# The inverse standard deviation of nine layer norms: Ln and Exp on rows, or Sqrt and reciprocal on tokens

## The chip, the cores and the metric

One core of one Trainium2 chip runs the whole program in one launch. The metric is the device time of that core in microseconds (us), the median of the runs. Engines are named as in the profile: PE (TensorE), PEld (its weight loads), DVE (VectorE), ACT (ScalarE), POOL (GpSimd) and SP (SyncE).

## The reference, cut to what matters

A small transformer-like network over 4 x 1024 tokens of 128 features. Each of its eight blocks is added to the residual and takes a layer norm of it without gain or bias; one norm more, over 256 features, sits inside the seventh block.

```python
def _layernorm(x, axis=-1, eps=1e-05):
    m = jnp.mean(x, axis=axis, keepdims=True)
    v = jnp.var(x, axis=axis, keepdims=True)
    return (x - m) / jnp.sqrt(v + eps)

x = x + _L0_attn_ref(_layernorm(x), ...)   # attention, 16 heads of 8, softmax
x = x + _L0_ffn_ref(_layernorm(x), ...)    # mixture of experts, the best 2 of 8
x = x + _L1_attn_ref(_layernorm(x), ...)   # attention
x = x + _L1_ffn_ref(_layernorm(x), ...)    # experts with a capacity, best 1 of 8
x = x + _L2_attn_ref(_layernorm(x), ...)   # state-space scan
x = x + _L2_ffn_ref(_layernorm(x), ...)    # mixture of experts, the best 2 of 16
x = x + _L3_attn_ref(_layernorm(x), ...)   # scan; inside: yn = (y - mu) / sqrt(var + 1e-05) * ln_g + ln_b
x = x + _L3_ffn_ref(_layernorm(x), ...)    # squared relu, then five spike steps
```

## The kernel before

The residual lies in SBUF as `g.xT`, features on the 128 partitions and the 4096 tokens along them; a norm writes `g.xn`. The program is a series of stages (class `Stage`), each with semaphores and PSUM of its own, and each is one `nc.Block()`: one instruction list per engine, run in the order written, and a barrier of all engines at its end. The order inside a stage is written by hand; nothing plans it.

`norm_stage` is called nine times: n0 to n7 with one source tile (k = 1), n0 ahead of the first attention, n1 and n3 ahead of the expert stages `f0r` and `f1r`, n5 ahead of `f2r`; and `m3n` with two source tiles (k = 2), in place. Tokens are cut into eight chunks of 512 (`CH`), these into two halves m of four chunks q. Features are on the partitions, so sums over them are matmuls:

- `mean(c)`, L172: a 128x128 matrix of 1/(128 k) times chunk c puts the mean on all 128 partitions of a PSUM bank; three banks in turn.
- centring, L216 on DVE: source minus mean, into the destination.
- `square(c)`, L227 on ACT.
- `variance(m)`, L179 on PE: four matmuls with 32 output columns each, so that chunk q of the half has its variance on the 32 partitions of group q (the same row 32 times) of one bank.
- `inverse_root(m)`, ACT: L231 takes the Ln of variance plus eps, 128x512 out of PSUM, and L233 the Exp of minus one half of it, into `inv`.
- `broadcast(m)`, L190 on PE: four matmuls, a one-hot column of the identity against the 32 partitions of group q, spread the row of chunk q over 128 partitions. Half 0 goes to banks 5, 6, 7, 0, half 1 to banks 1 to 4.
- `scale(m)`, L211 on DVE: destination times these banks, 4 k multiplies of 128x512.

PE's order is `mean` 0 to 5, `variance(0)`, `mean` 6 and 7, `broadcast(0)`, `variance(1)`, `broadcast(1)`. DVE has the eight centrings, then `scale(0)`, `scale(1)`. ACT has squares 0 to 5, `inverse_root(0)`, squares 6 and 7, `inverse_root(1)`. Ahead of that ACT is told to load a table set that holds both functions, and warms it:

```python
act.preload_act_table_set("natural_log_exp_and_others")   # L235
act.activation(warm[:, :], g.eps[:, :], ACT.Ln).then_inc(table, 1)   # L236
```

Other loads of tables are placed by the compiler in front of an ACTIVATE whose function the set then loaded lacks. Outside the norms these lines use `Exp` first: L642 (a warm-up at the head of each of the two attention stages), L1153 (`f0r`), L1634 (`f1r`), L924 and L925 (`f2r`). L1328 is the first `Silu` of the stage behind `f0r`.

Other lines that the text speaks of: L822, `f0r` and `f1r`, transposes of 128x128 f32 on PE, four to a PSUM bank, read by DVE at L836; L133, a DVE copy of 128x512 f32 from PSUM; L903, a DVE reciprocal of 128x32.

Of the kernel before, what the change touches and what calls it, by code (L numbers as in the profile page):

```python
# [13 lines left out]
ACT = mybir.ActivationFunctionType  # L14
# [4 lines left out]
P = 128  # L19
BATCH, SEQ = 4, 1024  # L20
TOK = BATCH * SEQ
CH = 512
NCH = TOK // CH
# [113 lines left out]
def norm_stage(nc, g, name, src=None, dst=None, ahead=()):  # L137

    src, dst = src or [g.xT[:, :]], dst or [g.xn[:, :]]
    k = len(src)
    with Stage(nc, name) as s:
        sq = s.sb("sq", [P, k, TOK])
        mean_w = s.sb("mean_w", [P, P])
        log, inv, warm = s.sb("log", [P, 2, CH]), s.sb("inv", [P, 2, CH]), s.sb("warm", [P, 1])
        ps = s.ps("ps", [P, 8, CH])
        bank = lambda i: ps[:, i, :]
        mean_ps, var_ps = [bank(i) for i in range(3)], [bank(3), bank(4)]
        spread = [[bank(i) for i in (5, 6, 7, 0)], [bank(i) for i in (1, 2, 3, 4)]]  # L150
        w_ready, mean_ready, centred, squared = (s.sem(x) for x in ("w_ready", "mean_ready", "centred", "squared"))
        var_ready, log_done, inv_done, inv_spread, scaled, table = (
            s.sem(x) for x in ("var_ready", "log_done", "inv_done", "inv_spread", "scaled", "table"))
        cols = lambda c: slice(c * CH, (c + 1) * CH)
        group = lambda q: slice(32 * q, 32 * q + 32)
        with nc.Block() as block:
            @block.sync
            def _(sp):
                for weights in ahead:
                    weights.load(sp)  # L160

            @block.gpsimd
            def _(pool):
                pool.memset(mean_w[:, :], 1.0 / (k * P)).then_inc(w_ready, 1)  # L164

            @block.tensor
            def _(pe):
                def mean(c):
                    if c >= 3:
                        pe.wait_ge(centred, k * (c - 2))  # L170
                    for i in range(k):
                        mm = pe.matmul(mean_ps[c % 3], mean_w[:, :], src[i][:, cols(c)], start=i == 0, stop=i == k - 1)  # L172
                    mm.then_inc(mean_ready, 1)

                def variance(m):
                    pe.wait_ge(squared, 4 * k * (m + 1))
                    for i in range(k):
                        for q in range(4):
                            mm = pe.matmul(var_ps[m][group(q), :], mean_w[:, 0:32], sq[:, i, cols(4 * m + q)],  # L179
                                           start=i == 0, stop=i == k - 1)  # L180
                    mm.then_inc(var_ready, 1)

                def broadcast(m):
                    pe.wait_ge(inv_done, m + 1)
                    if m == 0:
                        pe.wait_ge(centred, k * 7)
                    else:
                        pe.wait_ge(centred, k * NCH)
                    for q in range(4):
                        mm = pe.matmul(spread[m][q], g.ident[group(q), 32 * q:32 * q + 1].to_broadcast([32, P]),  # L190
                                       inv[group(q), m, :], start=True, stop=True)
                    mm.then_inc(inv_spread, 1)

                pe.wait_ge(w_ready, 1)
                for c in range(6):
                    mean(c)
                variance(0)
                mean(6)
                mean(7)
                broadcast(0)  # L200
                variance(1)
                broadcast(1)

            @block.vector
            def _(dve):
                def scale(m):
                    dve.wait_ge(inv_spread, m + 1)
                    for q in range(4):
                        for i in range(k):
                            x = dst[i][:, cols(4 * m + q)]  # L210
                            dve.tensor_tensor(x, x, spread[m][q], ALU.mult).then_inc(scaled, 1)  # L211

                for c in range(NCH):
                    dve.wait_ge(mean_ready, c + 1)
                    for i in range(k):
                        dve.tensor_tensor(dst[i][:, cols(c)], src[i][:, cols(c)], mean_ps[c % 3], ALU.subtract).then_inc(centred, 1)  # L216
                dve.wait_ge(centred, k * NCH)
                scale(0)
                scale(1)
                dve.wait_ge(scaled, k * NCH)  # L220

            @block.scalar
            def _(act):
                def square(c):
                    for i in range(k):
                        act.wait_ge(centred, k * c + i + 1)
                        act.activation(sq[:, i, cols(c)], dst[i][:, cols(c)], ACT.Square).then_inc(squared, 1)  # L227

                def inverse_root(m):
                    act.wait_ge(var_ready, m + 1)  # L230
                    act.activation(log[:, m, :], var_ps[m], ACT.Ln, bias=g.eps[:, :]).then_inc(log_done, 1)  # L231
                    act.wait_ge(log_done, m + 1)
                    act.activation(inv[:, m, :], log[:, m, :], ACT.Exp, scale=-0.5).then_inc(inv_done, 1)  # L233

                act.preload_act_table_set("natural_log_exp_and_others")  # L235
                act.activation(warm[:, :], g.eps[:, :], ACT.Ln).then_inc(table, 1)  # L236
                for c in range(6):
                    square(c)
                inverse_root(0)
                square(6)  # L240
                square(7)
                inverse_root(1)


def store_stage(nc, g, out):
# [549 lines left out]
class Logits:  # L795
# [34 lines left out]
    def take(self, dve, link, L):  # L830
        for m in range(2):
            dve.wait_ge(self.logits, m + 1)
            for q in range(4):
                t = 16 * m + 4 * q
                from_q = self.tok_ps[:, m, :].rearrange("p (j q r) -> p q j r", q=4, r=32)[:, q, :, 0:self.e]
                last = dve.tensor_copy(L[:, t:t + 4, :], from_q)  # L836
            link(last)
# [1748 lines left out]
def build(nc, a, out):  # L2586
    with ExitStack() as ctx:
# [24 lines left out]
        with nc.sbuf_tensor("area0", [P, 9728], F32) as area0:  # L2612
# [27 lines left out]

            load_stage(nc, g, a["x"], a["ident"], (qkv0,))
            norm_stage(nc, g, "n0")
            attention(nc, g, "a0", qkv0, out0, True, HD ** -0.5, None, (out0, gate0))
            norm_stage(nc, g, "n1", ahead=(glu0,))
            with ExitStack() as kept:
                picked = Picked(nc, kept)
                pick_stage(nc, g, "f0r", gate0, picked)
                pick_glu_stage(nc, g, "f0", glu0, picked, (qkv1,))
            norm_stage(nc, g, "n2")
            attention(nc, g, "a1", qkv1, out1, False, HD ** -0.5 / P,  # L2650
                      SEQ / float(np.sqrt(SEQ - 1.0)) * SEQ ** -0.5 / P, (out1, gate1))
# [133 lines left out]
```

## Time and profile before

| | us |
|---|---|
| median of three runs | 3391.71 |
| lowest and highest | 3378.48, 3408.56 |
| the profiled execution | 3391.71 |
| its span in the trace | 3388.9 |
| ACT busy, DVE busy, PE busy | 1823.4, 2481.5, 2666.3 |

All times of the trace come from one execution, in us from the start of its span. A row of the timeline is: start, duration (of a merged group, from its first to its last moment), engine, line, operation, output and inputs, shape, count, and in brackets how long the engine sat idle before it and what ended that. A matmul of f32 with 512 columns shows as two records. The window view gives, for each stretch, its length, the busy time of each engine with the number of instructions, the mean granted TensorE clock (1.00 is 2.4 GHz, 0.50 is 1.2 GHz), the busy share of the DMA engines and GB/s.

### The profile page before, as it was taken

To read this page: it belongs to the slowest core of one execution; us is meant where nothing else is said; L and a number is where in the kernel's file an instruction comes from. 1 tells how busy PE (TensorE), PEld (TensorE's weight loads), DVE (VectorE), ACT (ScalarE), POOL (GpSimd) and SP (SyncE) were. 2 spreads that over 40 slices of the span, in tenths; PEclk is the share of its full clock that TensorE was granted. 3 is DMA by queue.
4 is the path that set the end of the run, shared out by engine and by line. 5 is a ranking of instruction groups with operands and counts; after the bars stand their busy time and mean duration, and the time that the engine had idled before them with its cause. 6 is when DMAs were issued, how large, how long until landed. Compare 5 with 4: busy or idle time off the path is not lost. (4 is left out here: it accounts for less than half of the span.)

```text
span 3388.9 us, 42668 instructions
## 1 busy us (share of the span) xinstructions
PE 2666.3 (79%) x12546; PEld 947.7 (28%) x12546; DVE 2481.5 (73%) x2890; ACT 1823.4 (54%) x3156; POOL 995.3 (29%) x1196
## 2 busy tenths in 40 slices
PE   6599999995578589999997418767777778996676
PEld 3122222222256212222221107322323223332222
DVE  6799999964255499999993642579999974446548
ACT  2388888883132358888886104355555531224333
POOL 4222222210554312222220036136777730000000
PEclk9599999998888779999998659888999999998778
DMA  3111111106333301111110402201000000001010
GB/s 101 50 29 25 23 27 25 23 15 155 43 92 95 103 17 24 28 24 23 26 26 25 122 22 69 65 25 40 13 6 13 6 1 0 0 0 61 13 37 25
DMA packets 165668, 128.48 MB, mean 38 GB/s; under 512 B 65341, under 2 KB 138941, under 8 KB 165296
## 3 DMA queue, kind: packets, MB, share of 16 engines
q1 hardware_dynamic: 129520, 85.31, 9.7%
q0 software_dynamic: 34880, 37.57, 4.0%
q10 hardware_dynamic: 1152, 4.19, 0.3%
q8 instruction: 56, 0.92, 0.1%
q14 instruction: 60, 0.49, 0.1%
HBM read 72.80 MB, written 54.09 MB: 37 GB/s over the span
## 5 line engine op out<-in xcount | busy, mean ns | idle before, releaser
L655 DVE TENSOR_REDUCE a_att_mx<-a_att_s 128x2 f32<-128x1024 f32 x1024 | 1204.8, 1219 | 59.8 <-PE a_att_s L566 47.5
L640 ACT ACTIVATE a_att_pt<-a_att_st 128x512 f32<-128x512 f32 x2048 | 1064.6, 602 | 243.5 <-PE a_att_st L592 242.8
L592 PE MATMUL a_att_st<-a_qst,a_kst 50*128 50x512 bf16 x2048 | 626.7, 388 | 61.8 <-ACT a_att_pt L640 50.4
L566 PE MATMUL a_att_s<-a_kst,a_qst 48*128 48x512 bf16 x2048 | 527.1, 400 | 79.1 <-PEq L306 46.2
L579 PE MATMUL a_att_av<-a_att_pt,a_att_vst 128*32 128x512 f32 x4096 | 554.2, 614 | 0.0
L592 PEld LDWEIGHTS a_att_st<-a_qst,a_kst 50*128 50x128 bf16 x2048 | 158.6, 94 | 733.6 <-ACT a_att_pt L640 675.8
L2218 POOL TENSOR_TENSOR g_xn<-m2s_hs,m2s_cb 128x1024 f32<-128x1024 f32 x128 | 300.8, 2355 | 119.0 <-DVE m2s_hs L2185 76.4
L2185 DVE TENSOR_TENSOR_SCAN m2s_hs<-m2s_da,m2s_bps 128x1024 f32<-128x1024 f32 x128 | 292.7, 2287 | 4.4
L493 POOL CAST a_att_mt_in<-a_att_nmax 128x16 bf16<-128x16 f32 x64 | 12.6, 197 | 937.1 <-DVE a_att_nmax L663 937.1
L2101 PE MATMUL m2s_yps<-g_xn,g_ident 128*128 128x512 f32 x512 | 242.9, 597 | 0.9
L2157 ACT COPY m2s_cb<-m2s_cps 128x1024 f32<-128x1024 f32 x128 | 129.5, 1012 | 183.9 <-POOL g_xn L2218 182.2
L566 PEld LDWEIGHTS a_att_s<-a_kst,a_qst 48*128 48x128 bf16 x2048 | 113.1, 94 | 231.9 <-DVE a_att_mx L655 169.7
L2180 DVE TENSOR_TENSOR m2s_bps<-m2s_dtx,m2s_bps 128x1024 f32<-128x1024 f32 x128 | 154.8, 1209 | 3.9 <-POOL m2s_dtx L2204 3.9
L164 POOL MEMSET n_mean_w<- 128x128 f32 x8 | 1.6, 204 | 526.8 <-POOLq L944 231.6
L2152 ACT ACTIVATE m2s_da<-m_dt,m2s_aneg 128x1024 f32<-128x1024 f32 x128 | 147.4, 1151 | 0.0
L2121 PE MATMUL m2s_bps<-m_bcs,m2s_sel 96*128 96x512 bf16 x256 | 79.2, 392 | 85.4 <-DVE m2s_hs L2185 82.8
L986 ACT ACTIVATE f_sg<-f_gp 128x512 f32<-128x512 f32 x72 | 43.0, 597 | 180.5 <-PE f_cp L975 180.5
L998 DVE TENSOR_TENSOR f_h<-f_sg,f_up 128x512 f32<-128x512 f32 x72 | 49.5, 688 | 120.8 <-ACT f_sg L986 120.8
L2101 PEld LDWEIGHTS m2s_yps<-g_xn,g_ident 128*128 128x128 f32 x512 | 97.0, 191 | 85.2 <-issue 63.9
L579 PEld LDWEIGHTS a_att_av<-a_att_pt,a_att_vst 128*32 128x32 f32 x4096 | 81.4, 108 | 131.9 <-issue 102.7
L235 ACT ACT_TABLE_LOAD x9 | 11.5, 1283 | 186.1 <-PEq L713 65.2
L1220 POOL DMA_INDIRECT f_back<-f_yr,f_to x78 | 74.7, 958 | 54.2 <-DVE f_yr L1414 32.0
(461 smaller groups left out, 3720.1 us busy)
## 6 DMA issues: line engine op xcount, KB each, us to landing
a_kstk<-a_qkv_part SPq DMA_DIRECT2D x64, 128.0 KB
f_xs<-f_sent SPq DMA_DIRECT2D x20, 396.0 KB, 4.1
a_qst<-a_qstk POOLq DMA_DIRECT2D x116, 64.0 KB, 2.3
a_kst<-a_kstk POOLq DMA_DIRECT2D x116, 64.0 KB, 2.4
a_qstk<-a_qkv_part SPq DMA_DIRECT2D x48, 128.0 KB, 2.2
f_sent<-f0r_zero SPq DMA_DIRECT2D x1, 5148.0 KB, 21.7
a_num<-a_att_oev SPq DMA_DIRECT2D x256, 16.0 KB
g_xn<-a_num ACTq DMA_DIRECT2D x8, 512.0 KB, 6.0
```

The lines of the kernel that those rows point to most:

```text
L566: mm = pe.matmul(s1[:, cut % 2, h, :], qst[u][64 * h:64 * h + SPECIAL, qt * P:(qt + 1) * P], kst[u][64 * h:64 * h + SPECIAL, kh * CH:(kh + ...
L579: mm = pe.matmul(av[32 * gr:32 * gr + 32, :], vst[u][:, kt, h, :], pt[:, 4 * (kt % 4) + 2 * half + h, :], start=kt == 0, stop=kt == 7)
L592: pe.matmul(st[:, e % 3, :], kst[u][64 * h:64 * h + STACK, kt * P:(kt + 1) * P], qst[u][64 * h:64 * h + STACK, half * CH:(half + 1) * CH], ...
L640: act.activation(pt[:, e % 16, :], st[:, e % 3, :], ACT.Exp, scale=scale).then_inc(exp_done, 1)
L655: dve.tensor_reduce(mx[:, par, 2 * cut:2 * cut + 2], s1[:, cut % 2, :, :], AX.X, ALU.max).then_inc(s1_used, 1)
L2101: mm = pe.matmul(yps[:, f, :], g.ident[:, :], hc[:, k % 4, f * CH:(f + 1) * CH], start=n == 0, stop=n == NS - 1)
L2121: mm = pe.matmul(bps[:, k % 2, f, :], sel[:, n:n + 1].to_broadcast([96, P]), bcs[:, (2 * (q // 2) + f) * CH:(2 * (q // 2) + f + 1) * CH], ...
L2152: act.activation(da[:, k % 4, :], dt[:, q % 2, span(q)], ACT.Exp, scale=aneg[:, q % 2, n:n + 1]).then_inc(da_done, 1)
L2157: act.copy(cb[:, k % 2, :], both(cps[:, :, :])).then_inc(c_copied, 1)
L2180: dve.tensor_tensor(over, dtx[:, q % 2, :], over, ALU.mult).then_inc(dbx_done, 1)
L2185: dve.tensor_tensor_scan(hs[:, k % 3, :], da[:, k % 4, :], over, 0.0, ALU.mult, ALU.add).then_inc(scan_done, 1)
L2218: pool.tensor_tensor(hc[:, k % 4, :], hs[:, k % 3, :], cb[:, k % 2, :], ALU.mult).then_inc(hc_done, 1)
```

## The change

Only `norm_stage` is edited. The variance still comes as rows, group q on 32 partitions. Instead of Ln and Exp on these rows, ACT copies them to SBUF (`take`), PE turns them with four transposes (`turn`), so that tokens are on partitions, ACT takes the square root of 128x16 values (`root`), DVE the reciprocal (`invert`) into a zeroed tile `inv` (one value in each 32), PE turns that back with four transposes (`turn_back`) into the variance's bank, DVE copies it to SBUF (`take_back`), and `broadcast` goes from there. Both halves are broadcast into the same four banks `row_ps`, which the means use too: `broadcast(0)` waits for all centrings, `broadcast(1)` for the multiplies of `scale(0)`. The orders of PE, DVE and ACT change as shown; POOL gets a memset of 128x1024; the table set is no longer named, and a one-element `Sqrt` stands first on ACT.

```diff
-        log, inv, warm = s.sb("log", [P, 2, CH]), s.sb("inv", [P, 2, CH]), s.sb("warm", [P, 1])
-        ps = s.ps("ps", [P, 8, CH])
-        mean_ps, var_ps = [bank(i) for i in range(3)], [bank(3), bank(4)]
-        spread = [[bank(i) for i in (5, 6, 7, 0)], [bank(i) for i in (1, 2, 3, 4)]]
+        rows, back = s.sb("rows", [P, 2, CH]), s.sb("back", [P, 2, CH])
+        std, inv = s.sb("std", [P, 2, 4, 4]), s.sb("inv", [P, 2, 4, 4, 32])
+        row_ps = s.ps("row", [P, 4, CH])
+        var_ps, tok_ps = s.ps("var", [P, 2, CH]), s.ps("tok", [P, 2, CH])
...
                 pool.memset(mean_w[:, :], 1.0 / (k * P)).then_inc(w_ready, 1)
+                pool.memset(inv[:, :, :, :, :], 0.0).then_inc(inv_set, 1)
...
+                def turn(m):
+                    pe.wait_ge(var_copied, m + 1)
+                    for j in range(4):
+                        mm = pe.transpose(tok_ps[:, m, j * P:(j + 1) * P], rows[:, m, j * P:(j + 1) * P], g.ident[:, :])
+                    mm.then_inc(tok_ready, 1)
+
+                def turn_back(m):
+                    pe.wait_ge(inv_ready, m + 1)
+                    for j in range(4):
+                        mm = pe.transpose(var_ps[:, m, j * P:(j + 1) * P],
+                                          inv[:, m, j, :, :].rearrange("p q r -> p (q r)"), g.ident[:, :])
+                    mm.then_inc(back_ready, 1)
+
                 def broadcast(m):
-                    pe.wait_ge(inv_done, m + 1)
+                    pe.wait_ge(back_copied, m + 1)
                     if m == 0:
-                        pe.wait_ge(centred, k * 7)
+                        pe.wait_ge(centred, k * NCH)
                     else:
-                        pe.wait_ge(centred, k * NCH)
+                        pe.wait_ge(scaled, 4 * k)
                     for q in range(4):
-                        mm = pe.matmul(spread[m][q], g.ident[group(q), 32 * q:32 * q + 1].to_broadcast([32, P]),
-                                       inv[group(q), m, :], start=True, stop=True)
-                    mm.then_inc(inv_spread, 1)
+                        mm = pe.matmul(row_ps[:, q, :], g.ident[group(q), 32 * q:32 * q + 1].to_broadcast([32, P]),
+                                       back[group(q), m, :], start=True, stop=True)
+                    mm.then_inc(rows_ready, 1)
...
                 variance(0)
                 mean(6)
                 mean(7)
+                turn(0)
+                variance(1)
+                turn_back(0)
+                turn(1)
                 broadcast(0)
-                variance(1)
+                turn_back(1)
                 broadcast(1)
...
+                def invert(m):
+                    dve.wait_ge(std_ready, m + 1)
+                    dve.wait_ge(inv_set, 1)
+                    dve.reciprocal(inv[:, m, :, :, 0], std[:, m, :, :]).then_inc(inv_ready, 1)
+
+                def take_back(m):
+                    dve.wait_ge(back_ready, m + 1)
+                    dve.tensor_copy(back[:, m, :], var_ps[:, m, :]).then_inc(back_copied, 1)
...
+                invert(0)
+                take_back(0)
+                invert(1)
                 dve.wait_ge(centred, k * NCH)
                 scale(0)
+                take_back(1)
                 scale(1)
...
-                def inverse_root(m):
+                def take(m):
                     act.wait_ge(var_ready, m + 1)
-                    act.activation(log[:, m, :], var_ps[m], ACT.Ln, bias=g.eps[:, :]).then_inc(log_done, 1)
-                    act.wait_ge(log_done, m + 1)
-                    act.activation(inv[:, m, :], log[:, m, :], ACT.Exp, scale=-0.5).then_inc(inv_done, 1)
-
-                act.preload_act_table_set("natural_log_exp_and_others")
-                act.activation(warm[:, :], g.eps[:, :], ACT.Ln).then_inc(table, 1)
+                    act.copy(rows[:, m, :], var_ps[:, m, :]).then_inc(var_copied, 1)
+
+                def root(m):
+                    act.wait_ge(tok_ready, m + 1)
+                    by_token = tok_ps[:, m, :].rearrange("p (j q r) -> p j q r", q=4, r=32)
+                    act.activation(std[:, m, :, :], by_token[:, :, :, 0], ACT.Sqrt, bias=g.eps[:, :]).then_inc(std_ready, 1)
+
+                act.activation(std[:, 0, 0, 0:1], g.eps[:, :], ACT.Sqrt).then_inc(table, 1)
+                act.wait_ge(table, 1)
                 for c in range(6):
                     square(c)
-                inverse_root(0)
+                take(0)
                 square(6)
                 square(7)
-                inverse_root(1)
+                root(0)
+                take(1)
+                root(1)
```

## Rows read from the trace of the kernel before

**Rows 1.** The head of the page

```profile
span 3388.9 us, 42668 instructions
```

**Rows 2.** Windows over norm stages, n1 and n7: length, busy times, clock, DMA

```profile
809.30:825.60 16.30, 11.67 (x48) 3.84 (x48) 10.47 (x16) 9.05 (x14) 0.20 (x1) 0.99 0.87 186
...
3265.10:3283.30 18.20, 13.58 (x48) 4.63 (x48) 10.46 (x16) 9.05 (x14) 0.20 (x1) 0.88 0.00 1
```

**Rows 3.** Timeline of n1: start, duration, engine, line, what, idle before

```profile
809.31 1.28 ACT L235 ACT_TABLE_LOAD   x1 [32.63 <-PEq L713]
...
810.60 0.20 ACT L236 ACTIVATE n_warm<-g_eps 128x1 f32<-128x1 f32 x1
...
814.91 1.07 PE L179 MATMUL n_ps<-n_sq,n_mean_w 128*32 128x512 f32 x8
...
815.91 1.98 PE L172 MATMUL n_ps<-g_xT,n_mean_w 128*128 128x512 f32 x4
...
819.18 2.48 DVE L211 TENSOR_TENSOR g_xn<-g_xn,n_ps 128x512 f32<-128x512 f32 x4 [0.56 <-PE n_ps L190]
...
819.33 1.07 PE L179 MATMUL n_ps<-n_sq,n_mean_w 128*32 128x512 f32 x8 [0.29 <-ACT n_sq L227]
...
820.47 0.69 ACT L231 ACTIVATE n_log<-n_ps,g_eps 128x512 f32<-128x512 f32 x1 [1.19 <-PE n_ps L179]
...
821.87 1.14 PE L190 MATMUL n_ps<-n_inv,g_ident 32*128 32x512 f32 x8 [1.47 <-ACT n_inv L233]
823.07 2.48 DVE L211 TENSOR_TENSOR g_xn<-g_xn,n_ps 128x512 f32<-128x512 f32 x4 [1.42 <-PE n_ps L190]
```

**Rows 4.** Timeline of the ends of n0 and of n5

```profile
23.85 1.06 PE L179 MATMUL n_ps<-n_sq,n_mean_w 128*32 128x512 f32 x8 [0.29 <-ACT n_sq L227]
...
26.38 1.93 PE L190 MATMUL n_ps<-n_inv,g_ident 32*128 32x512 f32 x8 [1.47 <-ACT n_inv L233]
28.36 2.48 DVE L211 TENSOR_TENSOR g_xn<-g_xn,n_ps 128x512 f32<-128x512 f32 x4 [2.18 <-PE n_ps L190]
...
2777.17 1.58 PE L190 MATMUL n_ps<-n_inv,g_ident 32*128 32x512 f32 x8 [1.47 <-ACT n_inv L233]
```

**Rows 5.** Timeline of `m3n`, both variances and the second half's multiplies

```profile
3191.96 1.92 PE L179 MATMUL m3n_ps<-m3n_sq,m3n_mean_w 128*32 128x512 f32 x16
...
3193.81 3.70 PE L172 MATMUL m3n_ps<-m_xs,m3n_mean_w 128*128 128x512 f32 x8
...
3199.55 1.92 PE L179 MATMUL m3n_ps<-m3n_sq,m3n_mean_w 128*32 128x512 f32 x16 [0.97 <-ACT m3n_sq L227]
...
3204.16 4.87 DVE L211 TENSOR_TENSOR m_xs<-m_xs,m3n_ps 128x512 f32<-128x512 f32 x8 [0.41 <-PE m3n_ps L190]
```

**Rows 6.** Timeline of `f1r`, from PE alone and from DVE alone: transposes and their reader

```profile
1907.40 1.41 PE L822 MATMUL f1r_gate_tok<-g_ident,f1r_gate_rows 128*128 128x128 f32 x8
...
1908.17 0.48 DVE L836 COPY f1r_L<-f1r_gate_tok 128x32 f32<-128x32 f32 x4 [5.33 <-PE f1r_gate_tok L822]
```

**Rows 7.** Line L133: duration ns min/median/max, first and last start, forms

```profile
L133 DVE COPY g_xT<-load_ps x8: 679/691/692, 7.1 to 12.6; 128x512 f32<-128x512 f32 x8
```

**Rows 8.** Timeline of `f2r`: the first Exp and the reciprocal

```profile
2797.29 0.23 ACT L924 ACTIVATE f2r_w<-f2r_m 128x32 f32<-128x32 f32 x1 [10.79 <-DVE f2r_ex L896]
...
2798.79 0.35 DVE L903 RECIPROCAL f2r_w<-f2r_tmp 128x32 f32<-128x32 f32 x1
```

**Rows 9.** Windows of 1.2 us, from 0.7 us behind the end of n1 and n3

```profile
826.20:827.40 1.20, 1.20 (x6) 0.56 (x10) 0.69 (x2) 0.00 (x0) 0.86 (x5) 0.50 0.00 0
...
1903.50:1904.70 1.20, 0.85 (x7) 0.30 (x11) 0.00 (x0) 0.00 (x0) 1.19 (x2) 0.68 0.00 0
```

**Rows 10.** Timeline behind `f0r`: a table load and the ACTIVATE it serves

```profile
865.22 1.28 ACT L1328 ACT_TABLE_LOAD   x1 [22.72 <-PEq L1050]
...
869.05 0.60 ACT L1328 ACTIVATE f_sg<-f_za 128x512 f32<-128x512 f32 x1 [2.54 <-PE f_zb L1246]
```

**Rows 11.** Timeline of ACT: the first Exp of `f0r` and of `f1r`

```profile
838.06 0.23 ACT L1153 ACTIVATE f0r_w<-f0r_m 128x32 f32<-128x32 f32 x1 [1.35 <-DVE f0r_m L1113]
...
1912.18 0.42 ACT L1634 ACTIVATE f1r_ex<-f1r_ex 128x256 f32<-128x256 f32 x1 [4.08 <-DVE f1r_ex L1549]
```

## What I expect of the change, and why

> **What bounds the kernel now.** I read the page first. Its head gives the span, 3388.9 us [rows 1], and the profiled execution is itself the median of the runs shown (3391.71 us), so the sum below is made against the span and carried over with the 2.8 us that lie around it. The program is a series of stages with a barrier of all engines between them, so no engine's share says what a stage is worth; the change touches one stage form, `norm_stage`, which runs nine times: eight with one source tile (k=1; I call them n0 to n7 by their names) and once with two (k=2, `m3n`). The windows over the norm stages give their lengths: 16.3 us for a typical one, 18.2 us for n7, which ran at a mean granted clock of 0.88 where n1 had 0.99 [rows 2]. All nine together take 163 us, 4.8% of the span. Nothing else is edited, so everything hangs on the end of each norm: its last VectorE multiply opens the barrier.
>
> Then the timeline of n1, a typical one [rows 3]. The reader should see that its last part is a chain without slack. I call S the moment at which the second variance starts (PE L179, 819.33), released by the last square. From S: 1.14 us to Ln (820.47), 1.40 us for Ln and Exp to the broadcast (PE L190, 821.87), 1.20 us to the first multiply of `scale(1)` (823.07), and 2.48 us for four multiplies, end at 825.55. Sum 6.22 us. The first half of the scaling (819.18, 2.48 us) is done in the shadow of this chain: it starts 0.15 us before S and is over 1.4 us before `scale(1)` may start. That overlap is what the change has to keep or lose.
>
> **The change up to S.** The means, the centring and the squares keep their order, banks and operations. `Ln`+`Exp` of half 0 leave ScalarE and a copy takes their place, in a gap in which ScalarE then waits for VectorE anyhow; the four transposes of `turn(0)` stand on PE behind `mean(7)`, where the broadcast of half 0 stood. PE then waits for the last square in either kernel. The new memset (128x1024) is on POOL, which has one memset of 128x128 and 0.20 us in the whole stage [rows 2]; eight times that is 1.6 us, and its result is wanted some 10 us in. Without that cover it would cost those 1.6 us. So S stays: 0 us.
>
> **The change behind S.** The chain is now, half 0 first:
> - PE has the second variance in front of `turn_back(0)`. After the first variance the next matmul started 1.00 us later (814.91 to 815.91) [rows 3]. `root(0)` and `invert(0)` run beside this: the nearest small ones are an ACTIVATE of 128x32 with 0.23 us and a RECIPROCAL of 128x32 with 0.35 us [rows 8], theirs are 128x16, and with hand-overs of 0.06 us (as Exp's end at 821.81 to PE at 821.87) they are through by S+0.7. Cover 0.3 us; if they were slower, every tenth beyond S+1.0 would count.
> - four transposes until a reader may start: 0.77 us (1907.40 to 1908.17) [rows 6].
> - `take_back(0)`, a VectorE copy of 128x512 out of PSUM: 0.69 us [rows 7], then 0.06 us to PE.
> - broadcast to first multiply, 1.20 us, then `scale(0)`, 2.48 us [rows 3].
> - now what was parallel is serial. `take_back(1)` stands behind `scale(0)` on VectorE (0.69), and `broadcast(1)` writes the same four banks that `scale(0)` reads, so it waits for `scaled`: 0.06 us, then broadcast to multiply again, and 2.48 us of `scale(1)`.
>
> The second half's other steps (`take(1)`, `turn(1)`, `root(1)`, `invert(1)`) run beside the first: S+1.14 + 0.6 + 0.06 + 0.77 + 0.06 + 0.23 + 0.06 + 0.35 gives S+3.3, before `scale(0)` starts at S+3.7, and `turn_back(1)` behind `broadcast(0)` is ready near S+4.3, while VectorE comes for it at S+6.2. They cost nothing as long as they end before `scale(0)` does.
>
> For the last broadcast the clock matters. In n0 it took 1.98 us to the first multiply (26.38 to 28.36) where n1 took 1.20, and in n5 PE was 1.58 us busy with it against 1.14 [rows 4]. The new last broadcast falls 0.7 us behind the point where the stage ends today. At just that place I read the granted clock behind all nine norms: it is 0.50 in eight and 0.68 in the one behind n3; two of the nine stand in [rows 9]. PE had idled since the end of its last broadcast, and it will have idled there again (from about S+4.2 to S+6.9). So I take 1.98 us, the value at the lower level (1.2 GHz), with 1.20 at 2.4 GHz as the other end.
>
> Sum for k=1: 1.00+0.77+0.69+0.06+1.20+2.48+0.69+0.06+1.98+2.48 = 11.41 us against 6.22: **+5.19 us**, or +4.41 at full clock. n0 took 7.00 us behind its S (23.85 to 30.84) [rows 4], so +4.41; n5 was 0.43 slower than n1, so +4.76. Six others at 5.19 make 31.1; together **40.3 us**.
>
> `m3n`: eight multiplies of 4.87 us in all per half, and PE goes on 1.85 us after a variance (3191.96 to 3193.81). Before, S to end was 9.48 us (3199.55 to 3209.03), the second broadcast hidden behind `scale(0)` [rows 5]. After: 1.85+0.77+0.69+0.06+1.20+4.87+0.69+0.06+1.98+4.87 = 17.04, so **+7.6 us**.
>
> **Table loads.** Each norm has a load in front today (809.31, 1.28 us), and the next ACTIVATE starts within 0.01 us of its end [rows 3]; with `Sqrt` first there will be one each too. But `natural_log_exp_and_others` also served the later `Exp` lines without a load, and a set loaded for `Sqrt` I take not to: five more, at L642 (twice), L1153, L1634 and L924. At L1328 the load sat right behind the barrier, ahead of the wait that its ACTIVATE carries (the ACTIVATE comes 2.5 us later) [rows 10]. If the new ones sit like that, they fit the idle time before those lines: 1.35, 4.08 us [rows 11] and 10.79 us [rows 8], the tightest with 0.07 us to spare; L642 is a warm-up at the head of a stage. Value taken 0; if a load came behind the wait it would be 1.28 us at each of three, 3.9 us, and 6.4 us for all five. The Trainium skill (ScalarE: Activation LUTs, "What ACT_TABLE_LOAD costs" and "Table sets: the hidden batching unit") puts a switch of sets at about 2.66 us, the load with a drain of 1.38 us, and says that exp followed by sqrt takes two loads. By it the five would be an estimated 13.3 us and the time about 3453; n1's load shows no such gap behind it.
>
> Sum: 40.3 + 7.6 = **+47.9 us**, 1.4%. Span 3388.9 to 3436.8, time 3391.7 to **3439.6 us**. The low end, the full clock at all nine last broadcasts, is nine times 0.78 us less: +41. The high end, half clock already at the first broadcast of n0 and n5 (their clock fell about there; 0.78 each) and the three loads exposed, is +53.
>
> **Rivals.**
> - *The loads are on the path.* For: 0.07 us of room at L1153. Against: the place of L1328's load. 3443.5 with three on the path, 3446 with all five. Chance 0.10. (By the Trainium skill's price of a switch, same page and section, this rival would stand at an estimated 3453.)
> - *It is not slower by 1%: the clock gives it back.* A norm that begins at the lower level is longer: n7 18.2 us against 16.3 [rows 2], 1.9 us. If the shifted ends made PE start each following stage at the upper level, nine times 1.9 us, 17 us, would come back: +31 us, 3422. It decides from 14 us, 1.6 us behind each norm. Against it: PE idles longer in the new tail, not less. Chance 0.08.
> - *The tail overlaps better than I read it*, the transposes and `take_back(0)` in half my 1.46 us, and the last broadcast at full clock: 9 x (0.73 + 0.78) = 13.6 us less, +34 us, 3426. Against: these durations are those of the same shapes [rows 6, 7]. Chance 0.07.
> - *The clock falls a step earlier*, so that `turn_back(0)` (at most 0.77 us more) and `broadcast(0)` (0.78 more) are slow in every norm: 9 x 1.55 = 14 us more, 3453.5. For: PE is less busy behind S than it was. Against: it still has its variance, transposes and broadcast up to S+4.2 without a gap of 1 us, and in seven of nine norms today's broadcast at S+2.5 to S+3.7 ran at full clock. Chance 0.09.
> - *The change does not do what it says* (faster, since Ln and Exp of 512 columns are gone): their 1.40 us leaves ScalarE, and 3391.7 - 9 x 1.4 = 3379 if the transposes were hidden. Against: `broadcast(1)` waits for `scaled`, whatever is cheap before it. Chance 0.01.
>
> **How the numbers follow.** My forecast has 0.65, and its own range is 3432 to 3445. The three runs of before lie from 3378 to 3409, so a median carries some 8 us of its own. The range takes in the +41 and +53 ends with that noise and reaches to the two smaller cases (3422, 3426) and most of the larger: 3419 to 3458. A change of under 1% (34 us) is about what a measurement of this kernel cannot tell from none. Slower by over 1%: forecast, loads and early clock are 0.84, and of the two cases at +31 and +34 (0.15 together) noise puts some on that side, less what it takes from the forecast: 0.86. Within 1%: 0.12. Faster: 0.02.
>
> **What would show it.** In the new profile: nine norms of 21.4 us (from 16.3), `m3n` 37 us (from 29.5); `scale(0)` starting 3.7 us behind the second variance, not 0.15 before it; a VectorE copy between the two groups of multiplies and 2 us of VectorE idle time released by PE behind it; five more table loads, with the idle time of VectorE behind L1153, L1634 and L925 unchanged (0.3, 0.5 and 0.8 us); all other stages within a few us of today. I am wrong if `scale(0)` still starts near S, if the second broadcast starts before `scale(0)` ends, or if stages between the norms move by more than the norms do.

## The result and the profile after

| | before | after |
|---|---|---|
| median, us | 3392.8 | 3426.4 |
| lowest and highest of eight | 3377.5, 3410.3 | 3421.5, 3435.6 |
| ratio, 95% interval | | 1.0100, 1.0077 to 1.0125 |

The changed kernel is 33.6 us slower, forecast was 47.9 us more; its 3426.4 us lie inside the range of 3419 to 3458. The execution that was profiled took 3451 us, more than any of the eight. Sixteen more executions of the changed kernel took 3418.4 to 3449.3 us; with them the median of 24 is 3423.7 us. The head of its profile, and its table loads (the count, busy us, mean ns, then the idle time ahead of them):

```profile
span 3449.3 us, 43078 instructions
...
L271 ACT ACT_TABLE_LOAD x9 | 11.5, 1283 | 183.3 <-PEq L751 64.7 <-PEq L1247 35.1 <-PEq L2121 20.4
```

To see where the time went I cut both traces at the barriers (the semaphore clears behind each). Nine norms took 167.0 us before and 211.9 us after, barrier to barrier: +44.9. One other stage differs by more than 10 us: the expert stage behind `f0r`, 235.9 against 268.6. It turned out to have nothing to do with the change (below).

The norm n1 after, its timeline from the last mean on; it answers to [rows 3]:

```profile
821.40 0.60 PE L188 MATMUL n_tok<-g_ident,n_rows 128*128 128x128 f32 x4
...
823.01 1.07 PE L181 MATMUL n_var<-n_sq,n_mean_w 128*32 128x512 f32 x8 [1.01 <-ACT n_sq L260]
...
823.15 0.26 DVE L228 RECIPROCAL n_inv<-n_std 128x16 f32<-128x16 f32 x1 [0.86 <-ACT n_std L269]
...
824.01 0.66 PE L194 MATMUL n_var<-g_ident,n_inv 128*128 128x128 f32 x4
...
824.70 0.69 DVE L232 COPY n_back<-n_var 128x512 f32<-128x512 f32 x1 [1.29 <-PE n_var L194]
...
825.44 1.14 PE L205 MATMUL n_row<-n_back,g_ident 32*128 32x512 f32 x8
...
826.72 2.48 DVE L238 TENSOR_TENSOR g_xn<-g_xn,n_row 128x512 f32<-128x512 f32 x4 [0.69 <-PE n_row L205]
829.12 0.68 DVE L232 COPY n_back<-n_var 128x512 f32<-128x512 f32 x1
...
829.86 1.14 PE L205 MATMUL n_row<-n_back,g_ident 32*128 32x512 f32 x8 [2.69 <-DVE n_back L232]
831.06 2.48 DVE L238 TENSOR_TENSOR g_xn<-g_xn,n_row 128x512 f32<-128x512 f32 x4 [1.26 <-PE n_row L205]
```

The second variance (S) starts at 823.01. The first multiplies start 3.71 us behind it, where they stood 0.15 us ahead of it before; then the copy, the broadcast (PE idle for 2.69 us in front of it) and the second multiplies follow one by one, to S+10.53. Before, the end was at S+6.22.

n2 shows the same chain where the clock had fallen; only the last broadcast differs, 2.16 us to the first multiply instead of 1.20, as in [rows 4]:

```profile
1156.77 2.09 PE L205 MATMUL n_row<-n_back,g_ident 32*128 32x512 f32 x8 [2.69 <-DVE n_back L232]
1158.93 2.48 DVE L238 TENSOR_TENSOR g_xn<-g_xn,n_row 128x512 f32<-128x512 f32 x4 [2.21 <-PE n_row L205]
```

And `m3n`, second variance at 3250.60, with both halves of multiplies and the broadcast between them; it answers to [rows 5]:

```profile
3255.17 4.87 DVE L238 TENSOR_TENSOR m_xs<-m_xs,m3n_row 128x512 f32<-128x512 f32 x8 [0.69 <-PE m3n_row L205]
3259.96 0.68 DVE L232 COPY m3n_back<-m3n_var 128x512 f32<-128x512 f32 x1
3260.70 2.09 PE L205 MATMUL m3n_row<-m3n_back,g_ident 32*128 32x512 f32 x8 [5.07 <-DVE m3n_back L232]
3262.85 4.87 DVE L238 TENSOR_TENSOR m_xs<-m_xs,m3n_row 128x512 f32<-128x512 f32 x8 [2.21 <-PE m3n_row L205]
```

From S to the end that is 17.12 us, 7.65 more than before. Another 0.90 us lie ahead of S: this `m3n` began with the granted clock at 0.50 (3229.6 to 3234.0).

### The profile page after: what moved, and what is told of

Its sections match the earlier page's. It is cut to its first block and busy times, and to the rows that moved or that the text cites. A ratio compares the mean times of both kernels' runs of the same rounds, so it can differ in the third digit from the quotient of the medians.

```text
span 3449.3 us, 43078 instructions
## 1 busy us (share of the span) xinstructions
PE 2678.1 (78%) x12690; PEld 960.5 (28%) x12690; DVE 2495.4 (72%) x2926; ACT 1819.0 (53%) x3161; POOL 1003.2 (29%) x1205
```

## The experiments

My theory 1: the cost is the tail of each norm, made of the late first half and a serial second half, and a norm's length goes into the time one for one. Rivals: table loads; the bank wait by itself; stages that give time back. The kernels ran in three groups, each on one chip beside the kernel before: e1 to e4, e5 to e8 and e9 to e12. "Norms" is the sum of the nine, barrier to barrier, from each kernel's one trace; "attentions" are the two long attention stages of that trace. The diffs below leave out the declarations of tiles.

| kernel | norms, us | expert stage | attentions | median against before, us | ratio, 95% |
|---|---|---|---|---|---|
| before, three traces | 167.0, 169.8, 169.0 | 235.9, 269.5, 236.1 | 673/683, 674/691, 691/673 | | |
| after | 211.9 | 268.6 | 673/674 | +33.6 | 1.0077-1.0125 |
| e3 after again | 210.4 | 270.2 | 673/683 | +34.3 | 1.0074-1.0122 |
| e1 parallel halves | 196.8 | 273.1 | 673/673 | +20.3 | 1.0040-1.0086 |
| e9 take_back on ACT | 208.2 | 236.6 | 691/683 | +47.9 | 1.0102-1.0184 |
| e2 delay only | 209.7 | 272.0 | 673/673 | +38.4 | 1.0089-1.0136 |
| e5 tables only | 165.8 | 266.9 | 673/674 | +12.5 | 0.9986-1.0040 |
| e6 serial only | 167.9 | 266.0 | 691/674 | +7.6 | 0.9987-1.0035 |
| e7 after, PE busy | 209.1 | 267.6 | 681/681 | +45.0 | 1.0080-1.0146 |
| e8 before, PE busy | 170.0 | 271.6 | 674/673 | -7.5 | 0.9955-1.0004 |
| e10 fill 1 and 3 | 167.5 | 235.7 | 673/674 | -16.8 | 0.9928-0.9981 |
| e11 fill 1 and 2 | 165.7 | 236.2 | 674/673 | -9.8 | 0.9958-1.0014 |

**e3 and e4, e12: the same kernels again.**

> The changed kernel once more, unchanged, for a second trace and a second set of times on the chip that also runs the other kernels of this call. If the 33 us more in the expert stage behind f0r of the first trace belong to the change, they are there again; if they are one execution's, that stage takes 236 to 240 us as in the kernel before. Norms: 20.6 us at full clock and 21.3 to 21.9 where the last broadcast is at half clock, in other norms than in the first trace if the phase of the clock decides.

> The kernel before once more, unchanged, for a second trace: how far its stages outside the norms differ between two executions. If such spread is what lies between 45 us in the norms and 34 us in the time, single stages (the second attention, the expert stages, the last scan) differ by 3 to 10 us with no edit at all.

> The kernel before once more, unchanged, for a third trace. Theory: its norms take 16.7 us (barrier to barrier) or 17.2 to 18.7 where the clock was low, and the two attentions 673, 682 or 691 us each, by how long the clock is low in them; nothing else differs by more than 4 us.

The expert stage takes 266 to 273 us in all eight traces of the first two groups, with or without the change, and 235.7 to 236.6 in all four of the last: it goes with the chip or the session, not with the kernel. (The traced execution of the changed kernel had it long; its eight timed ones, 15 to 30 us shorter, evidently not.) The rows of its scattering DMAs, the kernel before in its first trace and in e4: the DMAs take the same time, the waits ahead of them differ.

```profile
L1220 POOL DMA_INDIRECT f_back<-f_yr,f_to x78 | 74.7, 958 | 54.2 <-DVE f_yr L1414 32.0
```

```profile
L1220 POOL DMA_INDIRECT f_back<-f_yr,f_to x78 | 74.6, 957 | 87.7 <-DVE f_yr L1414 65.6
```

The lowest times of the kernel before follow: 3377 and 3376 us where the stage is short, 3411 and 3409 where it is long. Comparisons of times stand within one group for that reason. The attention stages have levels too, about 673, 681 to 683, and 691 us, in kernels with and without the change. The windows over the end of the second attention, first the kernel before (683 us), then the changed one (674): the granted clock there is 0.56 against 0.97.

```profile
1830.00:1857.00 27.00, 22.01 (x85) 2.83 (x77) 0.00 (x0) 11.70 (x23) 0.00 (x0) 0.56 0.02 4
```

```profile
1865.00:1892.00 27.00, 18.93 (x122) 4.26 (x122) 0.00 (x0) 19.95 (x39) 0.00 (x0) 0.97 0.03 6
```

The norms of e3 are 1.5 us from the first trace's in sum. Which of them are slow changes (n1 took 21.0 us between barriers there, 22.0 here) though the kernel is the same; what decides it no run shows.

**e1, the halves in parallel.**

```diff
+        spread = lambda m, q: row_ps[:, q, :] if m == 0 else (var_ps if q < 2 else tok_ps)[:, q % 2, :]
 # broadcast(m) writes spread(m, q), scale(m) reads it
-                    if m == 0:
-                        pe.wait_ge(centred, k * NCH)
-                    else:
-                        pe.wait_ge(scaled, 4 * k)
+                    pe.wait_ge(centred, k * NCH)
 # VectorE
-                take_back(1)
 # ScalarE, behind root(1)
+                act.wait_ge(back_ready, 2)
+                act.copy(back[:, 1, :], var_ps[:, 1, :]).then_inc(back_copied, 1)
```

> The changed kernel, with the second half's take_back on ScalarE behind root(1) and its broadcast into the four banks that are free by then (the variance's and the transposes'), so that it no longer waits for the first half's multiplies. Theory 1 (the cost is the serial second half plus the late first half): scale(1) follows scale(0) without a gap, a norm ends about 2.4 us later than in the kernel before instead of 4.3 to 5.3, m3n 4.8 instead of 8.5: 24 us in the nine norms instead of 45, so the time lies 20 us under the changed kernel's. Rival (the transposes and the copies themselves are the cost, or other stages are): under 5 us less than the changed kernel.

The time fell by 14.0 us against the changed kernel of the same group (3440.9 against 3454.9), the norms by 14 us as well. I had expected 20, but in this trace five norms were slow ahead of S, where the edit changes nothing: n0, n1, n4 and n7 reached it 1.6 to 3.0 us later than the usual 10.04, `m3n` 1.2 us later than 20.06; in e3 only n0 did, by 1.7. n2's timeline, second variance at 1155.91:

```profile
1158.35 1.14 PE L203 MATMUL n_row<-n_back,g_ident 32*128 32x512 f32 x8
...
1159.62 2.48 DVE L236 TENSOR_TENSOR g_xn<-g_xn,n_row 128x512 f32<-128x512 f32 x4 [0.69 <-PE n_row L203]
1160.11 0.58 ACT L279 COPY n_back<-n_var 128x512 f32<-128x512 f32 x1 [1.47 <-PE n_var L195]
...
1162.02 1.28 DVE L236 TENSOR_TENSOR g_xn<-g_xn,n_var 128x512 f32<-128x512 f32 x2
1163.22 1.28 DVE L236 TENSOR_TENSOR g_xn<-g_xn,n_tok 128x512 f32<-128x512 f32 x2
```

The second multiplies follow the first without a gap. At full clock such a norm is 18.61 us from its start to its last multiply, against 20.56 after and 16.25 before: of the 4.31 us, 1.95 are the serial second half, 2.36 the late first half, which the parallel halves keep. So both parts of theory 1 are real and of like size, and the rival that the serial half costs next to nothing is out.

**e9, the copy alone.** The diff is e1's without its first two hunks: `take_back(1)` on ScalarE, the bank and its wait as in the changed kernel.

> The changed kernel with take_back(1) moved from VectorE to ScalarE behind root(1), and the wait of broadcast(1) for the first half's multiplies kept: one of the two edits of the run with parallel halves. Theory 1: the copy (0.7 us) and its hand-over leave the chain, the broadcast still starts only when scale(0) ends, so a norm is about 0.75 us shorter than in the changed kernel, 6 to 7 us in all nine; the other half of what the parallel halves gave (13 to 14 us together) is the bank. Rival (the copy was the whole of it): 12 to 14 us less here too.

The time says nothing here: both attentions of the profiled execution were slow (691 and 683), the interval is wide, and no changed kernel ran in this group. The trace does. n2, second variance at 1138.27:

```profile
1141.98 2.48 DVE L238 TENSOR_TENSOR g_xn<-g_xn,n_row 128x512 f32<-128x512 f32 x4 [0.68 <-PE n_row L205]
1142.47 0.58 ACT L281 COPY n_back<-n_var 128x512 f32<-128x512 f32 x1 [1.46 <-PE n_var L194]
1144.61 1.14 PE L205 MATMUL n_row<-n_back,g_ident 32*128 32x512 f32 x8 [2.18 <-DVE g_xn L238]
1145.81 2.48 DVE L238 TENSOR_TENSOR g_xn<-g_xn,n_row 128x512 f32<-128x512 f32 x4 [1.34 <-PE n_row L205]
```

The copy is through at 1143.05, yet the broadcast starts at 1144.61, released by the multiplies. Second variance to end is 10.02 us, so moving the copy is worth 0.5 us a norm (I had said 0.75) and the bank the other 1.4.

**e6, the bank's wait alone, in the kernel before.**

```diff
                     else:
-                        pe.wait_ge(centred, k * NCH)
+                        pe.wait_ge(scaled, 4 * k)
```

> The kernel before with broadcast(1) waiting for the four multiplies of scale(0) as the changed kernel does, and nothing else. Theory 1 (that wait costs only because scale(0) is late): scale(0) ends 2.3 us behind the second variance and the inverse root is ready at 2.5, so the eight k=1 norms keep their length and m3n grows by about 0.9 us: time within 2 us of the kernel before. Rival (the wait is the cost by itself): 1.2 us and more in each norm, 11 us or more in all.

As theory 1 has it: the k=1 norms take 16.7 us between barriers, or 17.4 to 17.5 where the clock was low, as before. `m3n` has 31.9 instead of 30.0, 1.9 us more where I had said 0.9. Its last broadcast, first in e6 (second variance at 3234.22), then in the kernel before (3199.55):

```profile
3238.56 2.09 PE L190 MATMUL m3n_ps<-m3n_inv,g_ident 32*128 32x512 f32 x8 [2.42 <-DVE m_xs L211]
3240.71 4.87 DVE L211 TENSOR_TENSOR m_xs<-m_xs,m3n_ps 128x512 f32<-128x512 f32 x8 [2.29 <-PE m3n_ps L190]
```

```profile
3202.95 1.14 PE L190 MATMUL m3n_ps<-m3n_inv,g_ident 32*128 32x512 f32 x8 [1.47 <-ACT m3n_inv L233]
```

It starts at S+4.34 instead of S+3.40, released by the multiplies: that is the wait, 0.94 us, as expected. And from its start to the first multiply it takes 2.15 us instead of 1.21, since PE is busy with it for 2.09 us (half clock) instead of 1.14; that is the other 0.94. The ratio of the times is 1.0011, and 1.2 us in every norm (11 us, 0.3%) lies inside the upper end of its interval; it is the trace that excludes it. So the wait costs 1.4 us in a k=1 norm where the first half is late, and nothing where it is not.

**e5, the table loads alone.**

```diff
                 inverse_root(1)
+                act.activation(warm[:, 1:2], g.eps[:, :], ACT.Sqrt).then_inc(table, 1)
```

> The kernel before with a one-element Sqrt at the end of ScalarE's list in every norm (behind the last Exp, beside scale(1)). It brings a load for Sqrt in each norm's tail and the five loads at the Exp lines that the changed kernel has too, and no other difference. Theory 1 (loads sit ahead of the waits, in idle time): the norms keep their 16.3 us, VectorE's waits at the three router Exps stay 0.3, 0.5 and 0.8 us, the time is within 3 us of the kernel before. Rival (loads on the path): 4 to 6 us more for five of 1.28 us on the path, 18 us if the nine in the tails held up the barrier as well.

Fourteen loads more, as the table groups show (x9 in the norms' tails, then the five at the `Exp` lines, two of them at L643):

```profile
L243 ACT ACT_TABLE_LOAD x9 | 11.5, 1283 | 0.2
...
L643 ACT ACT_TABLE_LOAD x2 | 2.6, 1283 | 10.8 <-PEq L307 10.8
L1154 ACT ACT_TABLE_LOAD x1 | 1.3, 1283 | 0.0
...
L1635 ACT ACT_TABLE_LOAD x1 | 1.3, 1283 | 0.0
...
L925 ACT ACT_TABLE_LOAD x1 | 1.3, 1283 | 0.0
```

The three loads in the routers stand right behind the instruction ahead of them (no idle time), not behind the wait. The norms take 165.8 us in sum, fewer than in any trace of the kernel before, and `f0r`, `f1r` and `f2r` 39.0, 92.6 and 27.8 us against 39.2, 92.8 and 28.5. So the loads are off the path. The medians differ by 12.5 us, the ratio of 1.0013 leaves both signs open, and the lowest time is 5 us under the lowest of before: the traces settle this, the times alone would not.

**e2, a pure delay.**

```diff
                 scale(0)
+                for n in range(9):
+                    dve.tensor_copy(junk[:, :], spread[0][3]).then_inc(idled, 1)
+                    dve.wait_ge(idled, n + 1)
                 scale(1)
```

> The kernel before with nine VectorE copies of 128x512 between scale(0) and scale(1) in every norm: a pure lengthening, no table loads, no transposes, no other PSUM layout. A copy should take 0.73 us with its wait, of which 1.4 us in all fall into idle time, so a norm grows by about 5.2 us (m3n 6.6): 48 us in the norms. Theory 1 (a norm's length goes into the time one for one): the time is 44 to 50 us over the kernel before. Rival 1 (stages behind a norm give a part back, by the clock or a DMA that had more time): 30 to 38 us over it, as in the changed kernel (34 for 45 in the norms). Rival 2 (run-to-run spread of other stages hides it): the lowest times differ by 44 to 50 though the medians differ by less.

Norms 209.7 us, 41 more than the mean of the three traces of before (168.6); time +38.4 us (30 to 47 by the interval), the lowest times 44.3 apart. One for one within what can be measured. The changed kernel: norms +42.5 us (mean of two traces against mean of three), medians +33.6 and +34.3 (25 to 42 by the intervals), lowest times +44.0 and +38.4; by all 24 times of it the median is +30.9 and the lowest +40.9. 42.5 lies at the very end of the intervals, so one for one is likely for the change but not shown. A delay without tables, transposes or another PSUM layout costs as much as the change within this spread.

**e7 and e8, PE kept busy.**

```diff
 # e7, after
                 turn_back(1)
+                for _ in range(2):
+                    pe.matmul(tok_ps[:, 0, :], mean_w[:, :], sq[:, 0, cols(7)], start=True, stop=True)
                 broadcast(1)
 # e8, before
                 broadcast(1)
+                pe.wait_ge(scaled, 4 * k)
+                for _ in range(3):
+                    pe.matmul(bank(5), mean_w[:, :], sq[:, 0, cols(7)], start=True, stop=True)
```

> The changed kernel with two matmuls of 128x512 f32 (1.7 us at full clock) on PE between turn_back(1) and broadcast(1), where it idles for 2.7 us. Theory 1 with the clock: with PE busy the last broadcast runs at 2.4 GHz in all nine norms, so the norms at 21.3 to 21.9 us come down to 20.6: 3 to 6 us less in all. Rival (the level does not follow from that idle time): some norms still show 21.5, and where the clock is low the two matmuls hold the broadcast up by 0.5 to 1 us.

> The kernel before with three matmuls of 128x512 f32 (2.6 us at full clock) on PE beside scale(1), where it idles up to the barrier. If idle PE in a norm's tail is what makes the stage behind it start at 1.2 GHz, the first microseconds behind each norm are faster: up to 1 us a stage, 5 to 9 us less in all, and this kernel is under the kernel before. Rival (the level follows what came long before, or the matmuls end behind the multiplies where the clock is low): no gain, or up to 5 us more.

e7: the last broadcast takes 1.14 us in all nine norms, `m3n` included, where it took 1.56 to 2.09 in six of nine and in four of nine in the two traces of after. That is the theory's part. Of the eight k=1 norms five take 21.0 us between barriers, against three and three; n6 and n7 (22.75 and 22.95) were slow ahead of S, n5 (21.42) between S and its second broadcast. So the sum moved by only 1 to 3 us; for the time no changed kernel ran in this group to compare with. e8: the stages behind the norms start faster, the one behind n4 takes 50.9 instead of 52.6 us, the one behind n5 26.3 instead of 27.8 to 28.5; but n1 and n3 grew from 16.7 to 18.4. In n1 the last broadcast was at half clock (PE 2.00 us busy with it) and the three matmuls, 3.63 us, ended a microsecond behind the last multiply and held up the barrier; n3 has the same length.

**e10 and e11, the kernel before with PE kept busy on both sides of its last broadcast.**

```diff
                 variance(1)
+                pe.wait_ge(centred, k * NCH)
+                pe.matmul(bank(1), mean_w[:, :], sq[:, 0, cols(7)], start=True, stop=True)
                 broadcast(1)
+                pe.wait_ge(scaled, 4 * k)
+                for _ in range(3):      # e11: 2
+                    pe.matmul(bank(5), mean_w[:, :], sq[:, 0, cols(7)], start=True, stop=True)
```

> The kernel before with one matmul of 128x512 f32 on PE ahead of broadcast(1), beside Ln and Exp of the second half, and three behind it beside scale(1). The three alone gave faster first microseconds behind five norms and made two norms 1.6 us longer, where the clock had fallen ahead of broadcast(1). Theory: with PE busy ahead of it too, the clock holds, no norm grows and the gains stay: 8 to 12 us under the kernel before. Rival: the clock falls there anyway and the four matmuls hold up the barrier: no gain.

> As the run before, with two matmuls behind broadcast(1) instead of three: 0.9 us less PE work ahead of the barrier. If hold-ups at half clock were what limits, this is the better of the two by 1 to 3 us; if it is the clock at the start of the next stage, it is the worse one by up to 5 us.

e10 is 0.9954 of the kernel before (0.9928 to 0.9981), 16.8 us by the medians, the lowest median of all. The windows behind its norms n1 and n4, 1.2 us each from the barrier on, where before had 0.50 [rows 9], and its first copy in the stage behind n4:

```profile
825.00:826.20 1.20, 0.94 (x10) 0.58 (x14) 0.71 (x2) 0.00 (x0) 1.01 (x5) 1.00 0.00 0
...
2159.80:2161.00 1.20, 0.77 (x2) 0.49 (x3) 0.00 (x0) 0.00 (x0) 0.12 (x1) 1.00 0.00 0
```

```profile
2159.84 0.12 POOL L1881 MEMSET m2i_xb<- 128x24 f32 x1 [16.52 <-POOLq L156]
...
2161.52 1.53 DVE L1905 COPY m2i_xb<-m2i_ps 128x512 f32 x2 [2.16 <-PE m2i_ps L1895]
```

The clock is 1.00 in all seven windows read, and behind the norms of e8 and e11 too; the copy comes 1.7 us behind the stage's start (2.6 before), and the stage takes 50.8 instead of 52.6 us. In e10 and e11 the last broadcast takes 1.14 us in all nine norms, where two to four of nine were slower in the three traces of before; but e5, without such matmuls, had none slow either, so what the one matmul ahead of it does is likely and not shown. Six of the eight k=1 norms take 16.7 us between barriers, n7 its usual 18.7, and n6 grew to 18.4 as n1 did in e8. e11 shows the same stages at the same lengths, and its interval includes 1; whether two or three matmuls are better is open. About 8 us of the gain are seen in five stages behind norms (`f0r` lost 1 to 2); the rest of the 17 is not assigned, and the lowest times are 10 us apart. So some 8 us, 0.2%, have a cause in the traces; that the gain is 0.5% rests on one of three such kernels.

## Why the prediction was right, and where it was off

- *S stays, and what runs up to it.* Right where a norm starts at full clock: from the start to the second variance it is 10.04 us in n1 in both traces; `turn(0)` lies behind `mean(7)` and off the path. But that stretch has a clock of its own, which the forecast put at nothing: n7 began at 0.50 before and at 1.00 after and reached S 1.91 us sooner, `m3n` began at 0.50 after and reached it 0.90 us later. In e3 it was n0, 1.70 us later.
- *The chain behind S.* Right in order and nearly in size: forecast at full clock +4.41 us for a k=1 norm, measured 20.56 - 16.25 = +4.31 in n1, n4 and n6. The terms of n1: 1.00 (variance to transposes), 0.69 (transposes to copy, forecast 0.77), 0.69, 0.05, 1.28 (broadcast to multiply, forecast 1.20), 2.40, then 0.68, 0.06, 1.20 and 2.48. `m3n` grew by 7.65 us behind S, forecast 7.6.
- *That what was parallel is now serial.* Right, and e1 and e9 price it: 1.9 us a norm, of which 1.4 is the shared bank. e6 adds what I had not said: in a k=1 norm the wait for the bank is harmless unless the first half is late.
- *The clock at the last broadcast.* The idea was right, the size was not. I took 1.98 us at all nine since the windows at that place showed half clock in eight of nine norms before. In the trace after, n1, n4 and n6 had it at full clock (20.56 us). Nor is 1.98 the lower level, as I had called it: the clock fell within that broadcast of n0, and where it was low throughout it cost 2.16 us.
- *The sum of the norms.* Behind S the nine grew by 45.9 us where I had 47.9; ahead of it they became 1.0 us shorter (-1.91 and +0.90), which makes 44.9.
- *Table loads.* Right: five more (L680 twice, L1191, L1672, L962), VectorE's waits at the router Exps unchanged at 0.3, 0.5 and 0.8 us, and e5 with fourteen extra loads leaves every stage as it was. The load at L1191 ran at 844.2, its ACTIVATE at 845.6. The Trainium skill's 2.66 us for a switch of sets (ScalarE: Activation LUTs, "What ACT_TABLE_LOAD costs") showed in no stage here.
- *Sum against the median.* The forecast put the whole sum on the median: +47.9. The norms gave 42.5 to 44.9 us in the traces, the medians 34. e2, a delay of the same size, gave 38 and 44 (lowest times), so nothing in the change itself needs to give time back; the intervals reach to 42. The execution on which I based the sum had one attention stage at its middle level (683 us), and each of the three traces of the kernel before has one slow attention of two, the two traces of the changed kernel one of four. Whether the longer norms make that rarer, or two traces and a few times are too few, stays open.
- *The rivals and the range.* 3426.4 us lies in the wide range but outside my own of 3432 to 3445, and right where two rivals stood (3426 and 3422), so the time alone would speak for them; that it fell into the range owes something to the range's width. The traces speak against both. The tail did not overlap better: the transposes and the copy took 1.38 us of the 1.46, and the last broadcast was at full clock in three of nine norms. And the clock gave nothing back behind the norms: it was 0.50 over the first 1.2 us behind all nine in both traces of the changed kernel, no stage there was faster by more than 0.5 us in both, and `f1r` took 2 us more in both. That the clock falls a step earlier is out too: the first broadcast took 1.14 us in all nine norms of both traces. Whether "slower by over 1%" came true cannot be said, with a ratio of 1.0100 and an interval on both sides of it; but a change of that size can be told from none here, which I had doubted.

## What to carry to other kernels

When a barrier follows, price a change by the chain from the last input to the last store, and write down what is in the shadow of what: here 4.3 us a norm came from a first half that no longer ran beside that chain (2.4) and a second half that waited for it (1.9), while the busy times of PE, DVE and ACT moved by under 1%. A wait for a buffer can be worth nothing or its whole length by what comes before it, so test it in the schedule in which it will stand. And where a short stage ends with PE idle, a few matmuls into a free bank can cost less than the faster start of the next stage gives back, as long as they end before the barrier: in e10 about 8 us of 3390 came back, in e8 two norms grew by 1.6 us.

## What the runs showed of the hardware

- The TensorE clock behind the barriers: 0.50 behind eight of nine norms before, 1.00 in all seven windows read with four extra matmuls in the norm's tail. Five stages behind norms took 8 us less in all, 0.2% of the time.
- The same broadcast of four matmuls, 32 rows by 512 columns, keeps PE busy for 1.14 us at full clock and 2.09 at half; with two matmuls ahead of it, where PE idled before, it took 1.14 in all nine norms of e7.
- The attention stages take about 673, 682 or 691 us in the same kernel, with the granted clock at the stage's end low or not (0.56 against 0.97 over 27 us).
- The expert stage with its 78 scattering DMAs takes 236 us in some sessions and 266 to 273 in others, for every kernel; the DMA instructions themselves take 75 us in both, and the waits ahead of them 54 or 88 us.
- A load of an activation table cost nothing where it could start, in idle time, ahead of the wait that its ACTIVATE carries: fourteen extra loads of 1.28 us moved no stage. It does not always stand there: in the kernel before, the load at L2374 started only when ScalarE's wait of 2.48 us for PE had ended, at 3141.85, and its ACTIVATE followed at 3143.15.
